# A mixture-of-experts kernel on one core: 64 token tiles in place of 68, the last four with two experts each

## The chip, the cores and the metric

One NeuronCore of one Trainium2 chip. The metric is the device time of one execution in microseconds (us), median of three runs; lower is better.

## The reference

128 samples of 64 tokens and 256 features pass two conditional layers. Each sample names one of 8 experts for the first layer and one of 16 domains for the second. Cut to what matters:

```python
# layer 0: expert of the sample, D=256, I=1024
h = gelu(x[b] @ Wi[e[b]] + bi[e[b]])
r = h @ Wo[e[b]] + bo[e[b]] + x[b]
x = layernorm(r, 1e-12) * gamma[e[b]] + beta[e[b]]
# layer 1: adapter of width 64, domain of the sample
a = gelu(x @ down_W.T + down_b)
a = a @ expert_W[d[b]].T + expert_b[d[b]] + domain_emb[d[b]]
x = layernorm(a @ up_W.T + up_b + x, 1e-5) * ln_gamma + ln_beta
```

## The kernel before

The kernel first sorts the 128 samples on the chip. `count_i`, `two_pairs`, `key`, `place`, `first`, `where` and `slot` (L682 to L698) give every sample a slot so that the samples of one expert are neighbours, the expert with most samples first. A tile is two slots: 128 tokens on the partitions. **Both halves of a tile always have the same expert**, so an expert with an odd count leaves half a tile empty, and the program has a fixed `TILES = B // 2 + E0 // 2` = 68 tiles.

The weights of an expert come from HBM in 8 chunks of 128x512 float32. Each is split into two float16 parts, a high part by ACT (`high`, L518) and a low part by DVE (`low`, L737), and stays in the tiles `W`, at `place` of its expert. Expert 0's chunks are made before the first tile; one more chunk is made per step of the loop after that. A matmul uses high times high, high times low and low times high.

All engines run the same loop of `STEPS = TILES + 5` steps (`run`), each its own part, and wait for each other with semaphores. In step i, PE makes:

- the first product of tile i: 8 blocks `c` of 128 columns of I, 2 halves `k` of D, 3 matmuls each (48 matmuls of 128 moving columns, L929 to L931),
- with it the up product of tile i-4 (L958, L962) and the down product of tile i-3 (L948),
- the second product of tile i-1: L1028 for the bias and 8 blocks `j` times 3 matmuls (24 of 256 moving columns, L937 to L939), and in the middle the transpose of tile i-2 (L970).

ACT makes the Gelu of tile i in 8 blocks (L589), two high parts of it (L597), the turned and scaled `yT` (L629) and the adapter's Gelu (L613, L616). DVE makes the low parts (L775), residual, statistics and normalisation (L785 to L825). POOL makes the inverse roots (L488, L492), the multiplication by gamma (L483), the last scale and shift (L475, L477), and copies the small tables of the tile's expert (`gb_tile` L496, `bi_tile` L461, `sel_tile` L502). SP loads and stores.

Which expert a tile has is known on the chip only. So `W` is read at an address that PE's sequencer works out from registers: at the start of a step it loads four numbers of the tile (`indices`, L262), and `first_addresses` (L918) and `second_addresses` (L923) work out all weight addresses of a few blocks at once, ahead of the matmuls that use them (`pe.lower_ap`):

```python
if c in (1, 3, 5):
    first_addresses(here, range(c + 1, c + 3))
ins = first_product(parity, here, c)
...
    if c in (2, 4):
        second_addresses(there, range(2 * c - 4, 2 * c))
```

In `run`, 8 first steps are written out, 48 steps run in a loop with weights and 8 in a loop without (four steps a turn on PE), and the rest is written out.

Of the kernel before, what the change touches and what calls it, by code (L numbers as in the profile page):

```python
# [9 lines left out]
TILES = B // 2 + E0 // 2  # L10
SLOTS = 2 * TILES
ENTRIES = E1 + 2
# [8 lines left out]
LEAD = NCH  # L21
STEPS = TILES + 5

# [12 lines left out]
IDX_LEN = IDX_CHUNK + E0  # L36


def build(nc, t):
# [4 lines left out]
    with ctx:  # L44
# [36 lines left out]
        bi_tile = sb("bi_tile", [P, 2, KI])  # L81
# [7 lines left out]
        gb_tile = sb("gb_tile", [P, 2 * KD])  # L89
# [38 lines left out]
        before = early(6, SLOTS)  # L128
# [10 lines left out]
        row, empty = early(6, SLOTS)[0:1], early(7, SLOTS)[0:1]  # L139
# [12 lines left out]
        where = early(7, E0)  # L152
        placed = early(7, E0)
# [38 lines left out]
        dst_rows = sem("dst_rows")  # L192
# [39 lines left out]
        yT_done = sem("yT_done")  # L232
        yg_done = sem("yg_done")
# [42 lines left out]
        def run(eng, step, unroll=4, ahead=0):  # L276

            lead, mid = LEAD - ahead, CHUNKS - FIRST_CHUNKS - ahead
# [3 lines left out]
            tail = mid + (TILES - 2 - mid) // 4 * 4  # L282
            for begin, end, weights, times in ((lead, mid, True, unroll), (mid, tail, False, 4)):
                with eng.Fori(0, (end - begin) // times) as n:
                    i = eng.snap(n * times + begin)
                    for q in range(times):
                        step(i + q, q % 2, (begin + q) % 4,
                             (q, n + (FIRST_CHUNKS + LEAD) // NCH, (LEAD + q) % SLOTS_W) if weights else False)
            for i in range(tail, STEPS):
                step(i, i % 2, i % 4, False)  # L290

# [15 lines left out]
        def _(sp):  # L307
            AHEAD = 2
# [12 lines left out]

            def inside(b):
                return [nc.s_assert_within(r, 0, B - 1, skip_runtime_bounds_check_because="the sorting clips every index")
                        for r in b]
# [42 lines left out]
            def step(i, parity, four, weights):  # L367
# [4 lines left out]
                if exists(i + 2) or exists(i - 5):  # L372
                    b = indices(sp, 6 * i + IDX_SP, 6, SLOTS - 1)
                if exists(i + 2):
                    load_turned(inside(b[2:4]), i + 2, parity)
# [5 lines left out]
                if exists(i):  # L381
                    load_natural(inside(b[0:2]), i, parity)

            run(sp, step, NCH, AHEAD)

# [4 lines left out]
        def _(pool):  # L390
# [66 lines left out]

            def gather_bi(e, i, parity):

                need(pool, gelu_half, 2 * i - 2)  # L460
                pool.tensor_copy(bi_tile[:, parity, :], bi_c[:, bass.ds(e * KI, KI)]).then_inc(bi_done, 1)  # L461
# [3 lines left out]
            def step(i, parity, four, weights):  # L465
# [12 lines left out]
                if exists(i - 3):  # L478

                    if isinstance(i, int) and i == 3:  # L480
                        pool.wait_ge(g_in, 16)
                    pool.wait_ge(z1_done, i - 2)
                    pool.tensor_tensor(yg[:, 1 - parity, :], z1[:, :], g_t[:, bass.ds(e_third * D, D)], ALU.mult)\  # L483
                        .then_inc(yg_done, 1)
# [8 lines left out]
                if exists(i - 2):  # L493

                    need(pool, yT_done, i - 2)
                    pool.tensor_copy(gb_tile[:, :], gb_c[:, bass.ds(e_before * 2 * KD, 2 * KD)]).then_inc(gb_done, 1)  # L496
# [19 lines left out]
        def _(act):  # L516
# [64 lines left out]
            def gelu(i, parity, half):  # L581
# [6 lines left out]
                for c in range(half * KI // 2, (half + 1) * KI // 2):  # L588
                    ins = nc.scalar.activation(h[:, c, :], p_h[parity][:, c, :], ACT.Gelu,  # L589
                                               bias=bi_tile[:, parity, c:c + 1], scale=1.0 / (XS * WS))  # L590
                ins.then_inc(gelu_half, 1)

            def high_h(i, parity, half):
# [3 lines left out]
                nc.scalar.activation(h_hi[:, parity, cols_h, :], h[:, cols_h, :], ACT.Copy, scale=HS)\  # L597
                    .then_inc(hhi_half, 1)

            def step(i, parity, four, weights):  # L600
                if exists(i + 1):
                    high_x(i + 1, 1 - parity)
                if weights:

                    act.wait_ge(w_in[weights[2]], w_loads(i, weights[2]))
                    high(weights[0], weights[1], stage[:, weights[2], :]).then_inc(w_hi, 1)
# [11 lines left out]
                if exists(i):  # L618
                    gelu(i, parity, 0)
                    high_h(i, parity, 0)  # L620
# [3 lines left out]
                if exists(i - 2):  # L624
# [3 lines left out]
                    for k in range(KD):  # L628
                        ins = nc.scalar.activation(yT[:, k, :], p_t[:, k * P:k * P + P], ACT.Identity,  # L629
                                                   bias=gb_tile[:, KD + k:KD + k + 1], scale=gb_tile[:, k:k + 1])  # L630
# [7 lines left out]
        def _(dve):  # L638
# [43 lines left out]
            link(v.tensor_scalar(count_i[:, :], p_u[:, 0:E0], 1.0, None, ALU.add))  # L682
# [8 lines left out]
            v.tensor_scalar(idx[:, IDX_CHUNK:IDX_LEN], ord_f[:, :], float(NCH), None, ALU.mult).then_inc(idx_ready, 1)  # L691
# [9 lines left out]
            v.tensor_scalar(before[:, :], iota_r[:, :], slot[:, :], None, ALU.is_gt).then_inc(cols_ready, 1)  # L701
# [23 lines left out]
            n_sort[0] += 4  # L725
# [3 lines left out]
            v.tensor_copy(sel[:, :], p_o[:, 0:SLOTS]).then_inc(sel_ready, 1)  # L729

# [19 lines left out]
            for n, m in enumerate(FIRST_ORDER):  # L750
# [4 lines left out]
                if n == 3:  # L755
# [7 lines left out]
            dve.wait_ge(dst_rows, 1)  # L763
            link(v.tensor_tensor(row, iota_r[0:1, :], p_u[0:1, SLOTS:2 * SLOTS], ALU.subtract))
            link(v.tensor_scalar(empty, p_u[0:1, 0:SLOTS], -1.0, 1.0, ALU.mult, ALU.add))
            link(v.scalar_tensor_tensor(row, row, float(B), empty, ALU.add, ALU.mult))
            v.tensor_tensor(sp_idx[:, 5:TILES + 5, 4:6], row.rearrange("a (t n) -> a t n", n=2),
                            p_u[0:1, 2 * SLOTS:3 * SLOTS].rearrange("a (t n) -> a t n", n=2), ALU.add)\
                .then_inc(idx_ready, 1)

            def split_h(i, parity, half):
# [3 lines left out]
                v.scalar_tensor_tensor(h_lo[:, parity, cols_h, :], h[:, cols_h, :], HS, h_hi[:, parity, cols_h, :],  # L775
                                       ALU.mult, ALU.subtract).then_inc(hlo_half, 1)

            def step(i, parity, four, weights):
# [48 lines left out]
                if weights:  # L827

                    dve.wait_ge(w_hi, i + 1)
                    low(weights[0], weights[1], stage[:, weights[2], :]).then_inc(w_lo, 1)  # L830
# [8 lines left out]
        def _(pe):  # L839
# [36 lines left out]
            pe.wait_ge(cols_ready, 4)  # L876
# [36 lines left out]
            def first_addresses(place_reg, cs):  # L913

                for k in range(KD):
                    for c in cs:
# [171 lines left out]
```

## Time and profile before

| | |
|---|---|
| time, median of 3 runs (lowest to highest) | 499.21 us (498.99 to 499.26) |
| the profiled execution, its own time | 498.85 us |
| its span in the profile | 497.1 us |
| busy: PE, PE weight load, DVE, ACT, POOL | 95%, 88%, 72%, 75%, 72% |
| mean granted TensorE clock | 0.983 of full speed |

Times in rows are microseconds from the start of the span. PEld is the weight load of PE; PEldq, POOLq, ACTq, DVEq and SPq are the sequencers, which do register work and hand instructions to their engines. FUSED_REGOPS and ALU_OP are register instructions, TENSOR_LOAD fetches numbers from memory into registers. "issue" is idle time that no event of another engine explains.

### The profile page before, as it was taken

The numbers are of one execution on the slowest core, as the hardware profiler recorded it, in microseconds if no ns is written. First come the engines' busy times: TensorE is split into PE (matmuls) and PEld (weight loads), VectorE is DVE, ScalarE is ACT, GpSimd is POOL, SyncE is SP. The second block draws the span as 40 slices with busy tenths as digits, with TensorE's granted clock in tenths as the row PEclk, the third lists the DMA queues.
The fourth block names the chain that finished last, engine by engine and source line by source line (L and its number), as shares of the span: only waits on it lengthen the run. The fifth ranks groups of instructions, "written<-read, shape, count | busy, mean of one in ns | idle before, by whom it ended". The sixth has DMA issues, their size and how long they took to land.

```text
span 497.1 us, 19258 instructions
## 1 busy us (share of the span) xinstructions
PE 473.9 (95%) x5778; PEld 438.7 (88%) x5779; DVE 355.6 (72%) x936; ACT 373.8 (75%) x1099; POOL 358.6 (72%) x587
## 2 busy tenths in 40 slices
PE   4699999999999999999999999999999999999972
PEld 2399999999999999999999999999999999999961
DVE  6678777777777777777777777777777767666662
ACT  2588887777787778788777778877878877677651
POOL 6044787788778877788778877887778876667765
PEclk9799999999999999999999999999999999999996
DMA  4734343333343333333333333333343222222111
GB/s 117 269 83 117 93 91 105 100 95 99 102 106 105 86 99 100 98 96 103 103 88 95 99 100 99 102 86 102 97 100 79 63 55 66 64 58 55 39 44 32
DMA packets 70257, 45.84 MB, mean 92 GB/s; under 512 B 43969, under 2 KB 61778, under 8 KB 70098
## 3 DMA queue, kind: packets, MB, share of 16 engines
q1 hardware_dynamic: 69200, 45.25, 34.6%
q8 instruction: 15, 0.25, 0.2%
q10 hardware_dynamic: 1026, 0.21, 0.2%
q14 instruction: 16, 0.13, 0.1%
HBM read 36.51 MB, written 8.91 MB: 91 GB/s over the span
## 4 chain that ended last, share of the span: by engine, by line
PE 93%; DVE 3%; POOL 1%; issue 1%; DMA 0%; ACT 0%; POOLq 0%; DVEq 0%
PE p_h L929 13%; PE p_h L931 12%; PE p_h L930 12%; PE p_o L939 12%; PE p_o L938 12%; PE p_o L937 12%; PE p_d L948 7%; PE p_u L962 6%; PE p_t L970 3%; PE p_u L958 2%; PE p_o L1028 1%; PE p_h L872 1%; DVE W L737 1%; POOL y L475 0%; PE p_t L872 0%
## 5 line engine op out<-in xcount | busy, mean ns | idle before, releaser
L929 PE MATMUL p_h<-x_hi,W 128*128 128x128 f16 x1088 | 193.8, 220 | 0.0
L930 PE MATMUL p_h<-x_lo,W 128*128 128x128 f16 x1088 | 193.6, 220 | 0.0
L931 PE MATMUL p_h<-x_hi,W 128*128 128x128 f16 x1088 | 193.6, 220 | 0.0
L589 ACT ACTIVATE h<-p_h,bi_tile 128x128 f32<-128x128 f32 x544 | 152.6, 362 | 0.6 <-PE p_h L931 0.6
L938 PE MATMUL p_o<-W,h_hi 128*128 x544 | 148.3, 273 | 0.0
L939 PE MATMUL p_o<-W,h_lo 128*128 x544 | 148.3, 273 | 0.0
L937 PE MATMUL p_o<-W,h_hi 128*128 x544 | 148.3, 273 | 0.0
L492 POOL TENSOR_TENSOR rs<-mv,neg_half 128x1 f32<-128x1 f32 x68 | 59.7, 878 | 74.2 <-DVE mv L808 74.2
L929 PEld LDWEIGHTS p_h<-x_hi,W 128*128 x1088 | 107.0, 98 | 5.2 <-issue 3.8
L930 PEld LDWEIGHTS p_h<-x_lo,W 128*128 x1088 | 106.9, 98 | 2.1
L931 PEld LDWEIGHTS p_h<-x_hi,W 128*128 x1088 | 106.9, 98 | 0.0
L613 ACT ACTIVATE a<-p_d,downb 128x128 f32<-128x128 f32 x68 | 25.0, 367 | 90.0 <-PE p_d L948 90.0
L775 DVE SCALAR_TENSOR_TENSOR h_lo<-h,h_hi 128x512 f16<-128x512 f32 x136 | 91.1, 670 | 1.4 <-ACT h_hi L597 1.4
L597 ACT ACTIVATE h_hi<-h 128x512 f16<-128x512 f32 x136 | 86.1, 633 | 2.2
L502 POOL COPY sel_tile<-sel 128x128 f16 (+1 forms) x68 | 81.0, 1191 | 2.0 <-issue 2.0
L805 DVE SCALAR_TENSOR_TENSOR a1s<-a,a1s 64x128 f16<-64x128 f32 x68 | 19.7, 289 | 66.5 <-ACT a1s L616 66.4
L475 POOL TENSOR_TENSOR y<-y,lng 128x256 f32<-128x256 f32 x68 | 49.3, 726 | 20.5 <-DVE h_lo L775 18.7
L785 DVE SCALAR_TENSOR_TENSOR r<-p_o,x_nat 128x256 f32<-128x256 f32 x68 | 28.8, 424 | 44.2 <-PE p_o L939 44.1
L939 PEld LDWEIGHTS p_o<-W,h_lo 128*128 128x128 f16 x544 | 53.2, 98 | 6.2
L938 PEld LDWEIGHTS p_o<-W,h_hi 128*128 128x128 f16 x544 | 53.2, 98 | 6.2
L629 ACT ACTIVATE yT<-p_t,gb_tile 128x128 f32<-128x128 f32 x136 | 55.3, 461 | 3.7 <-PE p_t L970 2.1
L937 PEld LDWEIGHTS p_o<-W,h_hi 128*128 128x128 f16 x544 | 53.2, 98 | 4.7
(155 smaller groups left out, 814.3 us busy)
## 6 DMA issues: line engine op xcount, KB each, us to landing
stage<-in_w SPq DMA_DIRECT2D x56, 256.0 KB, 2.7
x_nat<-in_x SPq DMA_DIRECT2D x136, 64.0 KB, 2.1
out<-y SPq DMA_DIRECT2D x136, 64.0 KB, 2.0
x_T<-in_xT SPq DMA_DIRECT2D x134, 64.0 KB, 2.2
W<-in_w SPq DMA_DIRECT2D x8, 256.0 KB, 4.6
g_t<-in_gamma SPq DMA_DIRECT2D x1, 1024.0 KB, 7.8
W<-in_expert_W SPq DMA_DIRECT2D x2, 128.0 KB, 3.0
upT<-in_up_W SPq DMA_DIRECT2D x2, 64.0 KB, 2.7
```

What stands on the lines that cost most here:

```text
L492: pool.tensor_tensor(rs[:, 1:2], mv[:, 1, 1:2], neg_half[:, 0:1], ALU.pow).then_inc(rs2_done, 1)
L502: pool.tensor_copy(sel_tile[:, four, :].rearrange("p (n s) -> p n s", n=2), sel[:, bass.ds(2 * i, 2)].unsqueeze(2).to_broadcast([P, 2, S]))\
L589: ins = nc.scalar.activation(h[:, c, :], p_h[parity][:, c, :], ACT.Gelu, bias=bi_tile[:, parity, c:c + 1], scale=1.0 / (XS * WS))
L597: nc.scalar.activation(h_hi[:, parity, cols_h, :], h[:, cols_h, :], ACT.Copy, scale=HS)\
L629: ins = nc.scalar.activation(yT[:, k, :], p_t[:, k * P:k * P + P], ACT.Identity, bias=gb_tile[:, KD + k:KD + k + 1], scale=gb_tile[:, k:k ...
L775: v.scalar_tensor_tensor(h_lo[:, parity, cols_h, :], h[:, cols_h, :], HS, h_hi[:, parity, cols_h, :], ALU.mult, ALU.subtract).then_inc(hlo ...
L929: mm(p_h[parity][:, c, :], hi, x_hi[:, parity, k, :], start=(k == 0), stop=False)
L930: mm(p_h[parity][:, c, :], hi, x_lo[:, parity, k, :], start=False, stop=False)
L931: ins = mm(p_h[parity][:, c, :], lo, x_hi[:, parity, k, :], start=False, stop=(k == KD - 1))
L937: mm(p_o[:, 0:D], h_hi[:, parity, j, :], hi, start=False, stop=False)
L938: mm(p_o[:, 0:D], h_hi[:, parity, j, :], lo, start=False, stop=False)
L939: return mm(p_o[:, 0:D], h_lo[:, parity, j, :], hi, start=False, stop=(j == KI - 1))
```

## The change

The tiles become 64. Only whole pairs of one expert are put in the first 60 tiles (`PURE`); the samples that are left over when a count is odd (8 at most) fill the last four tiles (`MIXED`), two samples with an expert each. In those four tiles every operation that depends on the expert is done by halves of 64 tokens. Since fewer tiles come before an expert is needed, each weight chunk is made two steps earlier (`EARLY`), two chunks in each of the first two steps. The output row of a slot is now the row that its input came from, which takes three matmuls and four DVE operations out of the sort.

```diff
-TILES = B // 2 + E0 // 2
+TILES = B // 2
+MIXED = E0 // 2
+PURE = TILES - MIXED
+EARLY = 2
...
-        def run(eng, step, unroll=4, ahead=0):
+        def run(eng, step, unroll=4, ahead=EARLY, first_looped=LEAD):
+            lead, mid = first_looped - ahead, CHUNKS - FIRST_CHUNKS - ahead
...
+            with eng.Fori(0, (mid - lead) // unroll) as n:
...
+            for i in range(mid, STEPS):
                 step(i, i % 2, i % 4, False)
+        def chunks(i, weights):
+            if isinstance(i, int) and i < EARLY:
+                return [(2 * i + q, (2 * i + q, 1, 2 * i + q)) for q in range(2)]
+            return [(i + EARLY, weights)] if weights else []
+        def mixed(i):
+            return isinstance(i, int) and PURE <= i < TILES
+        def tokens(i):
+            return [(n, HALF[n]) for n in range(2)] if mixed(i) else [(0, slice(0, P))]
+        def h_parts(i, parity):
+            if not mixed(i):
+                return h_hi[:, parity, :, :], h_lo[:, parity, :, :]
...  (mixed: two zero-padded copies, in h_hi/h_lo and in the free stage)
         # sort, DVE
+            link(v.scalar_tensor_tensor(excess[:, :], two_pairs[:, :], -2.0, p_u[:, 0:E0], ALU.mult, ALU.add))
+            link(v.tensor_tensor(cube[:, :, :], ahead[:, :, :], rows(excess[:, :], E0), ALU.mult))
+            link(v.tensor_reduce(behind[:, :], cube[:, :, :], AX.X, ALU.add))
+            link(v.tensor_reduce(all_pairs[:, :], two_pairs[:, :], AX.X, ALU.add))
+            link(v.scalar_tensor_tensor(behind[:, :], behind[:, :], all_pairs[:, 0:1], two_pairs[:, :], ALU.add,
+                                        ALU.subtract))
+            link(v.tensor_tensor(left_over[:, :], p_o[:, 0:E0], two_pairs[:, :], ALU.is_ge))
+            link(v.tensor_tensor(left_over[:, :], left_over[:, :], behind[:, :], ALU.mult))
+            link(v.tensor_tensor(where[:, :], where[:, :], left_over[:, :], ALU.add))
-            v.tensor_scalar(before[:, :], iota_r[:, :], slot[:, :], None, ALU.is_gt).then_inc(cols_ready, 1)
         # sort, PE
-            mm(p_u[0:1, 0:SLOTS], cols[:, 1:2], at_slot[:, :], start=True, stop=True)
-            mm(p_u[0:1, SLOTS:2 * SLOTS], cols[:, 1:2], before[:, :], start=True, stop=True)
-            mm(p_u[0:1, 2 * SLOTS:3 * SLOTS], cols[:, 0:1], at_slot[:, :], start=True, stop=True).then_inc(dst_rows, 1)
         # PE
+            def first_addresses(places, cs):
+                if len(places) == 1:
...
+            def second_addresses(places, js):
+                if len(places) == 1:
...
+            def first_product(i, parity, places, c):
+                for n, mine in tokens(i):
+                    for k in range(KD):
+                        hi, lo = first_weights(places[n], c, k)
+                        out = p_h[parity][:, c, mine]
+                        mm(out, hi, x_hi[:, parity, k, mine], start=(k == 0), stop=False)
+                        mm(out, hi, x_lo[:, parity, k, mine], start=False, stop=False)
+                        ins = mm(out, lo, x_hi[:, parity, k, mine], start=False, stop=(k == KD - 1))
+            def second_product(i, parity, places, j):
+                h_high, h_low = h_parts(i, parity)
+                for n, place_n in enumerate(places):
...
+                    mm(p_o[:, 0:D], h_high[at], hi, start=False, stop=False)
+                    mm(p_o[:, 0:D], h_high[at], lo, start=False, stop=False)
+                    ins = mm(p_o[:, 0:D], h_low[at], hi, start=False, stop=(j == KI - 1 and n == len(places) - 1))
+                def places(tile, place_reg):
+                    return indices(pe, IDX_MIX + 2 * (tile - PURE), 2, PLACE_TOP) if mixed(tile) else [place_reg]
+                here, there = places(i, here), places(i - 1, there)
-                        pe.wait_ge(w_lo, i - 1)
+                        pe.wait_ge(w_lo, i + EARLY)
         # POOL
+            def experts(i, e):
+                return indices(pool, IDX_MIX_EXP + 2 * (i - PURE), 2, E0 - 1) if mixed(i) else [e]
...  (used for gamma, bi_tile and gb_tile; gamma in two halves of 64 partitions that wait for each other)
         # ACT, DVE: Gelu, yT, high and low parts in halves for a mixed tile
+                    for n, mine in tokens(i):
+                        ins = nc.scalar.activation(h[:, c, mine], p_h[parity][:, c, mine], ACT.Gelu,
+                                                   bias=bi_tile[:, parity, n, c:c + 1], scale=1.0 / (XS * WS))
+                if isinstance(i, int) and PURE <= i < PURE + 2:
+                    clear_others(i, parity)      # 4 memsets of the zero padding
```

## Rows read from the trace of the kernel before

**Rows 1.** The page: busy us, share of the span, instructions; then its chain.

```profile
PE 473.9 (95%) x5778; PEld 438.7 (88%) x5779; DVE 355.6 (72%) x936; ACT 373.8 (75%) x1099; POOL 358.6 (72%) x587
...
PE 93%; DVE 3%; POOL 1%; issue 1%; DMA 0%; ACT 0%; POOLq 0%; DVEq 0%
```

**Rows 2.** Windows of two steps: length, PE, PEld, DVE, ACT, POOL busy; clock; DMA.

```profile
242.02:248.70 6.68, 6.68 (x87) 6.33 (x85) 4.97 (x13) 5.49 (x17) 5.61 (x9) 1.00 0.36 98
416.40:423.27 6.87, 6.87 (x87) 6.31 (x84) 4.37 (x12) 5.08 (x16) 5.04 (x9) 1.00 0.27 67
```

**Rows 3.** Timeline of PE: start, duration, instruction.

```profile
24.30 0.31 PE L930 MATMUL p_h<-x_lo,W 128*128 128x128 f16 x1
24.41 0.31 PE L931 MATMUL p_h<-x_hi,W 128*128 128x128 f16 x1
...
241.91 0.27 PE L939 MATMUL p_o<-W,h_lo 128*128 x1
242.02 0.22 PE L929 MATMUL p_h<-x_hi,W 128*128 128x128 f16 x1
242.08 0.22 PE L930 MATMUL p_h<-x_lo,W 128*128 128x128 f16 x1
...
416.39 0.10 PEld L929 LDWEIGHTS p_h<-x_hi,W 128*128 x1
...
481.69 0.27 PE L939 MATMUL p_o<-W,h_lo 128*128 x1
```

**Rows 4.** By source line, 413 to 424 us: duration min/median/max ns, first and last start.

```profile
L262 PEldq TENSOR_LOAD <-idx x1: 1003/1003/1003, 414.7 to 414.7; - x1
...
L262 PEldq ALU_OP  x1: 36/36/36, 421.7 to 421.7; - x1
L262 PEldq TENSOR_LOAD <-idx x1: 1000/1000/1000, 421.8 to 421.8; - x1
L918 PEldq FUSED_REGOPS  x3: 60/74/74, 422.9 to 423.2; - x3
L1001 PEldq FUSED_REGOPS  x1: 74/74/74, 423.3 to 423.3; - x1
L929 PEld LDWEIGHTS p_h<-x_hi,W x1: 95/95/95, 423.3 to 423.3; 128*128 x1
```

**Rows 5.** Waits of PE's weight load: us in total, times, longest.

```profile
PEld p_h L929 <- issue: 3.8, 15, 0.7
```

**Rows 6.** By source line, whole run: counts, ns min/median/max.

```profile
L918 PEldq FUSED_REGOPS  x611: 42/74/79, 23.2 to 471.8; - x153
...
L518 ACT ACTIVATE W<-stage x56: 612/628/659, 25.5 to 390.1; 128x512 f32 x48, 128x512 f16<-128x512 f32 x8
L518 ACTq ALU_OP  x42: 35/35/35, 80.2 to 389.0; - x42
...
L518 ACTq FUSED_REGOPS  x6: 60/60/65, 73.6 to 342.3; - x6
...
L262 POOLq TENSOR_LOAD <-idx x71: 562/1174/1281, 13.5 to 484.5; - x71
```

**Rows 7.** Timeline of the sort's end, DVE and PE.

```profile
7.99 0.17 DVE L697 TENSOR_TENSOR W<-W 128x8 f32<-128x8 f32 x1
8.19 0.16 DVE L698 TENSOR_REDUCE slot<-W 128x1 f32<-128x8 f32 x1
...
10.42 1.52 PE L878 MATMUL p_d<-W,cols 128*1 128x136 f32 x6 [1.07 <-DVE W L713]
...
12.62 0.61 PE L882 MATMUL p_u<-W,cols 128*1 128x136 f32 x2
...
14.07 0.80 PE L872 MATMUL p_h<-upT,W 64*128 64x256 f32 x2
```

**Rows 8.** The chain that ended last, around 487 us: start, us, what.

```profile
487.11 0.68 POOL yg L483
487.79 0.89 issue
```

More of the change, by code:

```diff
@@ L152, in build @@
         where = early(7, E0)
+        excess = early(7, E0)
+        behind = early(7, E0)
+        left_over = early(7, E0)
+        all_pairs = early(7, 1)
         placed = early(7, E0)
@@ L281, in run @@
                 step(i, i % 2, i % 4, (j % NCH, (j + FIRST_CHUNKS) // NCH, j % SLOTS_W))
[L282 to L289, printed above, removed]
-                step(i, i % 2, i % 4, False)
+            with eng.Fori(0, (mid - lead) // unroll) as n:
+                i = eng.snap(n * unroll + lead)
+                for q in range(unroll):
+                    step(i + q, q % 2, (lead + q) % 4,
+                         (q, n + (FIRST_CHUNKS + first_looped) // NCH, (first_looped + q) % SLOTS_W))
+            for i in range(mid, STEPS):
+                step(i, i % 2, i % 4, False)
+        def chunks(i, weights):
[9 more added lines that the diff above has]
+                return h_hi[:, parity, :, :], h_lo[:, parity, :, :]
+            if parity:
+                return h_hi, h_lo
+            flat = stage[:, :, :].rearrange("p a b -> p (a b)").bitcast(f16)
+            return [flat[:, u * 2 * KI * P:(u + 1) * 2 * KI * P].rearrange("p (n c q) -> p n c q", n=2, c=KI)
+                    for u in range(2)]
         def loads(i, parity, each):
@@ L495, in step @@
                     need(pool, yT_done, i - 2)
-                    pool.tensor_copy(gb_tile[:, :], gb_c[:, bass.ds(e_before * 2 * KD, 2 * KD)]).then_inc(gb_done, 1)
+                    for n, e_n in enumerate(experts(i - 2, e_before)):
+                        ins = pool.tensor_copy(gb_tile[:, n, :], gb_c[:, bass.ds(e_n * 2 * KD, 2 * KD)])
+                    ins.then_inc(gb_done, 1)
                 if exists(i):
@@ L602, in step @@
                     high_x(i + 1, 1 - parity)
-                if weights:
-                    act.wait_ge(w_in[weights[2]], w_loads(i, weights[2]))
-                    high(weights[0], weights[1], stage[:, weights[2], :]).then_inc(w_hi, 1)
+                for j, (m, place_n, slot_n) in chunks(i, weights):
+                    act.wait_ge(w_in[slot_n], w_loads(j, slot_n))
+                    high(m, place_n, stage[:, slot_n, :]).then_inc(w_hi, 1)
                 if exists(i - 3):
@@ L619, in step @@
                     gelu(i, parity, 0)
+                    if isinstance(i, int) and i == PURE:
+                        act.wait_ge(w_lo, CHUNKS - FIRST_CHUNKS)
                     high_h(i, parity, 0)
@@ L826, in step @@
                                     ALU.subtract, ALU.mult).then_inc(z2_done, 1)
-                if weights:
-                    dve.wait_ge(w_hi, i + 1)
-                    low(weights[0], weights[1], stage[:, weights[2], :]).then_inc(w_lo, 1)
+                for j, (m, place_n, slot_n) in chunks(i, weights):
+                    dve.wait_ge(w_hi, j + 1)
+                    low(m, place_n, stage[:, slot_n, :]).then_inc(w_lo, 1)
+                if isinstance(i, int) and PURE <= i < PURE + 2:
+                    clear_others(i, parity)
                 if exists(i):
@@ L911, in second_weights @@
                 return chunk[:, bass.ds(place_reg + at, D)], chunk[:, bass.ds(place_reg + (at + D), D)]
-            def first_addresses(place_reg, cs):
-                for k in range(KD):
-                    for c in cs:
-                        for part in first_weights(place_reg, c, k):
-                            pe.lower_ap(part, for_matmul_weights=True)
-            def second_addresses(place_reg, js):
-                for j in js:
-                    for part in second_weights(place_reg, j):
-                        pe.lower_ap(part)
@@ new lines, in second_addresses @@
+            def second_addresses(places, js):
+                if len(places) == 1:
+                    for j in js:
+                        for part in second_weights(places[0], j):
+                            pe.lower_ap(part)
+            def first_product(i, parity, places, c):
+                for n, mine in tokens(i):
+                    for k in range(KD):
+                        hi, lo = first_weights(places[n], c, k)
[3 more added lines that the diff above has]
+                        ins = mm(out, lo, x_hi[:, parity, k, mine], start=False, stop=(k == KD - 1))
+                return ins
```

110 lines of the change are left out of this document (60 added, 50 removed).

## The prediction

> **What bounds the kernel now.** I read the page first, then windows of single steps, then PE's instructions one by one, and last the sequencers' own instructions by source line. The page says that PE is busy 95% of the span and carries 93% of the chain that ended last [rows 1]. The windows show how full a step is: 6.68 us, all of it PE, at granted clock 1.00, with DVE, ACT and POOL at 5.0, 5.5 and 5.6 us [rows 2]. In PE's timeline a matmul of 256 moving columns starts 0.109 us after the last one, one of 128 columns 0.055 us after it [rows 3]: columns at full clock and nothing between. So a tile less is 6.68 us less, and four are 26.7 us. What the change is worth hangs on what the four mixed tiles cost.
>
> The instructions by source line show a second stream that is nearly as full, PE's sequencer. At the turn of a loop it does a register instruction at 421.7 us, at 421.8 a load of the tile's numbers, and is not back before 422.9: 1.06 us per load. Three instructions of `first_addresses` follow from 422.9 to 423.2, 0.13 us each, and only at 423.3 comes the first weight load [rows 4]. PE's array hides all of this in a plain step because the sequencer is ahead: the load of a step starts at 414.7 us, and the array gets to that step at 416.39 [rows 3, 4], 1.7 us later. At a loop's turn even that is not enough: that step takes 6.87 us [rows 2], and PE's weight load waits 3.8 us in 15 pieces for "issue" [rows 5]. The trace so shows PE starved by its own sequencer already, by 0.2 us a turn.
>
> **The change, part by part. The plain tiles.** Tiles 0 to 59 stay as they are. `run` has 12 turns on PE where it had 14: -0.4 us at 0.2 a turn. PE's new wait for `w_lo` (i + EARLY) asks for a chunk that DVE makes in step i-1 ahead of the low part of h that PE waits for next, so it never ends last. The second chunk in steps 0 and 1 is 0.63 us more of ACT [rows 6] and about as much of DVE, in steps from which four linked DVE operations go (0.2 us each or more): 0, and 0.6 at most if they were late. SP's transfers stay two steps ahead of their use: 0.
>
> **The start.** DVE gets eight linked operations before `slot`, at the 0.2 us from L697 to L698 [rows 7], and loses one (L701), so L878 on PE starts 1.5 us later than 10.42. Behind it L882 to L884 go, 12.62 to 14.07, 1.45 us [rows 7]. The next link, L872, so starts at about 14.1 as before. +0.1; +1.5 if a late tile of x, which is loaded after the sort, becomes the last to come.
>
> **A mixed tile on PE's array.** Its first product has 96 matmuls of 64 columns where there were 48 of 128. No row shows 64 columns with float16 weights. Below stands half the price of 128, 0.028 us, above the full 0.055. I take 0.028: nothing in the spacing shows a price beside the columns. The second product has 48 matmuls of 256 columns, 5.2 us, where there were 24. With 1.4 us for the rest, the array needs 9.3 us a step (12.0 by the upper bound) where both its tiles are mixed.
>
> **A mixed tile on PE's sequencer.** `first_addresses` and `second_addresses` do nothing for two places. Each weight address is so worked out in front of the matmul that uses it: high and low for 8 blocks, 2 halves of D and 2 experts are 64 in the first product, and 32 in the second. Before, they came in bundles: 611 instructions for 68 x 32 addresses, 3.6 in one [rows 6]. Alone, each takes an instruction. The nearest row of that is ACT's weight conversion, which is not lowered ahead: 42 ALU_OP and 6 FUSED_REGOPS for 48 chunks [rows 6]. The price of one lies between its own duration, 0.036 us, and the 0.133 from one bundle to the next [rows 4]. I take 0.10 us (the light instruction at 421.7 is followed at 421.8; the first block of each expert needs three operations, 0.12): 6.6 us for 64. `places` adds two loads to a step with two mixed tiles, 1.06 us each. Handing over a matmul costs next to nothing, since six pairs pass between the bundle at 423.2 and that of L1001, with which the two are no farther apart than the others [rows 4].
>
> The Trainium skill has two rules here. TensorE: Matmul & The Clock Gate, in its section on the back-to-back issue gap, gives matmuls of 1 to 64 columns some 60 cycles, about 25 ns. The first product of a mixed tile would be 2.4 us by it, if nothing but the array counted; no row here shows such a matmul. Its table also gives TensorE's queue 64 entries, 32 pairs, an estimate of 3.5 us of lead at 0.109; the trace has 1.7 us, and by 3.5 the sum below would come out some 3.5 us lower.
>
> **The sum.** Time 0 is where the array begins step 60 (423.3 us in the trace of before). The sequencer is at -1.7. Step 60: two loads 2.1, 64 addresses 6.6, the addresses of the plain second product 0.6, up product, waits and pairs 0.9: the first product is handed over at 8.5, and the array ends it with it. Its plain second product takes 2.9, so the step ends at 11.4 with the sequencer again 1.7 ahead. Steps 61 to 63: three loads 3.2, 64 addresses 6.6, rest 0.8, together 10.6, then 5.5 for the array's second product; less the lead of 1.7 that is 14.4 a step, 43.3 in all: 54.7. In the second product 32 addresses (3.3) lie under 5.5 of the array. Step 64: two loads and the rest, 2.9 less 1.7, then 5.5: 61.4. In the trace of before the same stretch, to the last second product of tile 67, is 423.3 to 482.0 [rows 3, 4] (the last L939 starts at 481.69 and ends at 482.0): 58.7. So +2.7.
>
> **The end.** After that, the chain runs through POOL [rows 8]. For mixed tiles POOL loads two more numbers for `gb_tile` in the one step and for gamma in the next, 1.17 us each [rows 6], and gamma is two operations of 0.7 in place of one, linked by a semaphore. The load of `gb_tile` puts y L475 off by 1.4, gamma's load shows by some 0.5 behind y L477, the second half by 0.8: +2.7; 0.8 if the loads hid, 4.0 if nothing did.
>
> Total: -0.4 + 0.1 + 2.7 + 2.7 = +5.1 us. The profiled execution took 498.85 us, 1.75 more than its span and 0.36 less than the median; I add to the median: 504.3 us.
>
> **The rivals.** (a) *The addresses are cheap or are hidden*, and the mixed steps go at the pace of another resource. For it speaks that register instructions last 36 to 79 ns and that the whole program shows just 3.8 us of starving [rows 4, 5]; against it, that three bundles and a load starve the array already. POOL would bind: four loads of 1.17, its 5.0 us of a step [rows 2], 0.7 for gamma and an estimated 0.5 for the small copies make 11 us in place of 14.4 in three steps, and step 60 gives 2.5: 12.6 less, 491.7 us. If POOL's loads hid too, the array's 9.3 a step would give 486; its upper bound, 12.0, gives 495. This is the side where the skill's 25 ns would put it. It decides where an address costs less than 0.08 us: 256 addresses in first products, 5.1 us between them and no change.
>
> (b) *The clock falls.* The array works 2.7 of some 10 us while it is fed by addresses. At half clock (0.11 us for 128 columns [rows 3]) the second product takes 10.6, the lead is worth 3.4, a step 17.8: 16 more if it stays so throughout, 520; 512 if it returns half the time. For it speaks that PE's gaps are new, against it that the gaps are short, 0.1 us between one matmul group and the next.
>
> (c) *The forecast's mechanism with another price*: 0.133 an address gives 513, 0.09 gives 502.
>
> **How the numbers follow.** Forecast (sequencer binds at 0.09 to 0.13 us): 0.58, range of its own 499 to 512. Rival (a): 0.29. Rival (b): 0.11, rest 0.02. A change below 0.2% (1 us) is what a measurement of this kernel can't tell. Slower: nearly all of the forecast (0.51) and (b), together 0.62; within 0.2%: 0.05 from the forecast's edge; faster: (a) and the low edge, 0.33. The range 488 to 513 leaves out (a) with all hidden (0.08), the clock down throughout (0.05) and the dearest address (0.04).
>
> **What would show it.** In the profile after: steps 60 to 63 of about 11, 14, 14 and 14 us where plain steps are 6.68; PE and PEld idle for "issue" in groups at L929 to L931's successors, 20 us or more in all; some 64 register instructions per mixed tile at the line of the first weights, 0.1 us apart; PE's share of busy time below 93%; POOL no longer than 11 us in such a step; the chain after the last second product some 3 us longer. Wrong it would be if the mixed steps were 9 to 11 us with POOL or the array without a gap, if the address instructions came bundled, or if the granted clock fell to half in 430 to 485 us.

## The result and the profile after

The changed kernel takes 507.0 us, the median of 4 runs (506.4 to 509.0), against 499.2 us (499.0 to 499.6) of the kernel before on the same chip: a ratio of 1.016 (95% interval 1.014 to 1.017). It is slower, by 7.8 us where 5.1 were forecast. Its profiled execution took 508.95 us with a span of 506.6.

The page of the changed kernel, busy time by engine, the granted clock in 40 slices, and the chain that ended last:

```profile
PE 479.4 (95%) x5724; PEld 437.3 (86%) x5725; DVE 341.7 (67%) x910; ACT 362.5 (72%) x1087; POOL 343.9 (68%) x567
...
PEclk9999999999999999999999999999999999889896
...
PE 90%; DVE 3%; issue 2%; POOL 2%; ACT 2%; DMA 0%; POOLq 0%; DVEq 0%; ACTq 0%
```

PE still looks 95% busy, as before [rows 1], and it has 5.5 us more busy time with 54 matmuls fewer. The slices show what is new: from the 35th on, the clock is no longer whole (the last slice was below whole in the kernel before too).

Windows of the changed kernel tell where the time is (columns as in [rows 2]). The first row is a plain step. The next five run from one step's bias matmul (L1113, between first and second product) to the next, from step 59 to 64; the last row is all that follows the last second product.

```profile
417.54:424.21 6.67, 6.67 (x87) 6.26 (x84) 4.36 (x12) 4.88 (x16) 5.00 (x10) 1.00 0.27 67
...
421.26:433.13 11.87, 11.25 (x135) 9.68 (x133) 7.37 (x22) 6.48 (x23) 6.92 (x14) 0.96 0.21 51
433.13:445.96 12.83, 12.36 (x132) 10.19 (x133) 5.36 (x19) 6.50 (x26) 4.39 (x9) 0.90 0.11 28
445.96:462.08 16.12, 15.38 (x157) 12.76 (x157) 4.96 (x15) 6.50 (x26) 4.83 (x11) 0.90 0.07 18
462.08:476.78 14.70, 13.94 (x156) 12.02 (x157) 4.26 (x13) 6.70 (x26) 4.72 (x10) 0.99 0.08 21
476.78:485.02 8.24, 8.23 (x60) 6.62 (x61) 0.86 (x3) 3.64 (x14) 2.46 (x4) 0.81 0.07 18
...
490.80:506.60 15.80, 4.42 (x25) 2.62 (x25) 6.04 (x18) 2.64 (x8) 8.64 (x15) 0.70 0.14 33
```

Plain steps are what they were. From mark to mark, a step with a mixed first product takes 11.9 to 16.1 us, about twice a plain one. In the one of 16.12 us POOL works 4.83 and ACT 6.50: neither binds. From the start of step 60 (424.21) to the end of the last second product (490.80) it is 66.6 us, against 58.7 before. These 7.9 us are most of the 9.5 by which the two profiled spans differ.

What PE's sequencer did in the mixed tiles, by source line, from 424 us to the end (duration min/median/max ns, first and last start). First the lines of two of the three matmuls, then, for 451 to 453 us, the loads at the start of step 62, one of four numbers and two of two numbers each:

```profile
L1006 PEldq ALU_OP  x95: 32/32/36, 424.3 to 476.3; - x95
L1006 PEldq FUSED_REGOPS  x32: 42/46/51, 424.1 to 472.2; - x32
...
L1008 PEldq ALU_OP  x96: 32/32/32, 424.4 to 476.5; - x96
L1008 PEldq FUSED_REGOPS  x32: 46/46/51, 424.2 to 472.4; - x32
```

```profile
L274 PEldq TENSOR_LOAD <-idx x3: 532/533/1002, 451.2 to 452.8; - x3
```

That is 255 instructions, each in front of one matmul (256 by count, 64 for each mixed tile). What they do to the array is seen in the timeline of PE's weight load in step 62 (start, duration), the first instructions after the three loads:

```profile
453.53 0.10 PEld L1006 LDWEIGHTS p_h<-x_hi,W 128*128 x1 [0.54 <-issue]
453.54 0.10 PEld L1007 LDWEIGHTS p_h<-x_lo,W 128*128 x1
453.65 0.10 PEld L1008 LDWEIGHTS p_h<-x_hi,W 128*128 x1
453.74 0.10 PEld L1006 LDWEIGHTS p_h<-x_hi,W 128*128 x1
453.77 0.10 PEld L1007 LDWEIGHTS p_h<-x_lo,W 128*128 x1
453.86 0.10 PEld L1008 LDWEIGHTS p_h<-x_hi,W 128*128 x1
454.00 0.10 PEld L1006 LDWEIGHTS p_h<-x_hi,W 128*128 x1
```

Three matmuls need two addresses (L1007 uses the weights of L1006). The six from 453.53 to 454.00 take 0.47 us, so an address costs 0.117 us; later in the product it is 0.11. Against that, the first mixed matmuls of step 60, in PE's timeline:

```profile
424.21 0.19 PE L1006 MATMUL p_h<-x_hi,W 128*128 128x64 f16 x1
424.24 0.19 PE L1007 MATMUL p_h<-x_lo,W 128*128 128x64 f16 x1
424.31 0.20 PE L1008 MATMUL p_h<-x_hi,W 128*128 128x64 f16 x1
```

Two matmuls of 64 columns start 0.03 us apart where no address lies between them, half of the 0.055 for 128 [rows 3]; the third waits for its address. At that spacing the array could do a group of three in 0.085 us (an estimate); it gets one every 0.22 to 0.23. Note that each still shows a duration of 0.19 us: durations overlap and fill the gaps, which is why the busy share hides the starving. Starts tell it, durations don't. The list of PE's waits has the same blind spot; of idle time for "issue" it names little more than these:

```profile
PEld p_h L1006 <- issue: 6.0, 20, 0.8
...
PEld p_u L1039 <- issue: 4.0, 8, 1.2
```

And the clock, in the timeline of a second product of 256 columns, where [rows 3] has 0.11 us from one start to the next:

```profile
434.36 0.42 PE L1019 MATMUL p_o<-W,h_lo 128*128 x1
434.57 0.42 PE L1017 MATMUL p_o<-W,h_hi 128*128 x1
```

0.21 us: half clock. In this execution it is so in three stretches of 3.4 us, from 432.2, 445.8 and 476.5 us. Windows of the first one and of the mixed first product ahead of it:

```profile
424.21:432.20 7.99, 7.45 (x99) 6.44 (x98) 4.44 (x14) 3.56 (x14) 3.97 (x9) 1.00 0.18 45
432.20:435.60 3.40, 3.32 (x22) 2.40 (x22) 1.03 (x4) 1.74 (x8) 2.13 (x3) 0.50 0.20 43
```

Each stretch begins 0.2 to 0.9 us ahead of the bias matmul of its step (60, 61 and 63), so near the end of a mixed first product.

The start and the end. In the sort, PE's timeline has

```profile
11.08 0.59 PE L940 MATMUL p_t<-W,cols 128*1 128x128 f32 x2 [3.32 <-DVE W L767]
...
14.73 2.08 PE L947 MATMUL p_h<-upT,W 64*128 64x256 f32 x8
```

where L947 is the L872 of before at 14.07 [rows 7]: +0.7. After the last second product the chain has on POOL (start, duration), and POOL's own timeline beside it:

```profile
492.38 0.55 POOL rs L535
492.93 0.48 issue
493.42 0.51 POOLq L274
```

```profile
493.45 0.61 POOL L539 TENSOR_TENSOR rs<-mv,neg_half 128x1 f32<-128x1 f32 x1 [0.52 <-DVE mv L882]
494.09 0.47 POOL L544 COPY gb_tile<-gb_c 128x4 f32 x2
```

The load of the two experts' numbers for `gb_tile` takes 0.51 us, not 1.17. The chain is led through it, but it ends at 493.93, and POOL is busy with L539 until 494.06, so it delays `gb_tile` by nothing. Gamma's two halves are not in the chain at all. The end is 15.8 us against 15.1.

### The profile page after: what moved, and what is told of

It is laid out like the page before. It is cut to its first block, busy times and chain, and to the rows that moved or that the text cites. A ratio compares the mean times of both kernels' runs of the same rounds, so it can differ in the third digit from the quotient of the medians.

```text
span 506.6 us, 19097 instructions
## 1 busy us (share of the span) xinstructions
PE 479.4 (95%) x5724; PEld 437.3 (86%) x5725; DVE 341.7 (67%) x910; ACT 362.5 (72%) x1087; POOL 343.9 (68%) x567
## 4 chain that ended last, share of the span: by engine, by line
PE 90%; DVE 3%; issue 2%; POOL 2%; ACT 2%; DMA 0%; POOLq 0%; DVEq 0%; ACTq 0%
PE p_h L1006 13%; PE p_h L1008 12%; PE p_o L1017 12%; PE p_o L1018 12%; PE p_o L1019 12%; PE p_h L1007 11%; PE p_d L1029 6%; PE p_u L1043 5%; PE p_t L1051 3%; PE p_u L1039 2%; PE p_o L1113 2%; PE p_h L947 1%; DVE W L810 0%; ACT h L639 0%; ACT ctab L591 0%
## 5 line engine op out<-in xcount | busy, mean ns | idle before, releaser
L1006 PE MATMUL p_h<-x_hi,W 128*128 128x128 f16 (+1 forms) x1088 | 193.3, 216 | 1.3 <-issue 0.8
L1008 PE MATMUL p_h<-x_hi,W 128*128 128x128 f16 (+1 forms) x1088 | 193.3, 216 | 0.0
L1007 PE MATMUL p_h<-x_lo,W 128*128 128x128 f16 (+1 forms) x1088 | 193.1, 216 | 0.0
L639 ACT ACTIVATE h<-p_h,bi_tile 128x128 f32<-128x128 f32 (+1 forms) x544 | 148.7, 359 | 5.3 <-PE p_h L1008 5.3
L1017 PE MATMUL p_o<-W,h_hi 128*128 x512 | 140.2, 274 | 0.0
L1018 PE MATMUL p_o<-W,h_hi 128*128 x512 | 140.1, 274 | 0.0
L1019 PE MATMUL p_o<-W,h_lo 128*128 x512 | 140.0, 273 | 0.0
L1006 PEld LDWEIGHTS p_h<-x_hi,W 128*128 x1088 | 106.4, 98 | 10.0 <-issue 6.0
L1007 PEld LDWEIGHTS p_h<-x_lo,W 128*128 x1088 | 106.3, 98 | 1.9
L539 POOL TENSOR_TENSOR rs<-mv,neg_half 128x1 f32<-128x1 f32 x64 | 55.1, 861 | 73.5 <-DVE mv L882 73.5
L843 DVE SCALAR_TENSOR_TENSOR h_lo<-h,h_hi 128x512 f16<-128x512 f32 (+1 forms) x128 | 83.4, 654 | 1.9 <-ACT h_hi L650 1.8
L650 ACT ACTIVATE h_hi<-h 128x512 f16<-128x512 f32 (+1 forms) x128 | 78.9, 619 | 2.0
L686 ACT ACTIVATE yT<-p_t,gb_tile 128x128 f32<-128x128 f32 (+1 forms) x136 | 54.0, 455 | 12.8 <-PE p_t L1051 10.9
L535 POOL TENSOR_TENSOR rs<-mv,neg_half 128x1 f32<-128x1 f32 x64 | 35.5, 554 | 36.8 <-DVE mv L871 36.8
L1018 PEld LDWEIGHTS p_o<-W,h_hi 128*128 128x128 f16 x512 | 50.3, 98 | 6.1
```

Source lines behind the costliest of these rows:

```text
L539: pool.tensor_tensor(rs[:, 1:2], mv[:, 1, 1:2], neg_half[:, 0:1], ALU.pow).then_inc(rs2_done, 1)
L639: ins = nc.scalar.activation(h[:, c, mine], p_h[parity][:, c, mine], ACT.Gelu, bias=bi_tile[:, parity, n, c:c + 1], scale=1.0 / (XS * WS))
L650: ins = nc.scalar.activation(out, h[:, cols_h, mine], ACT.Copy, scale=HS)
L686: ins = nc.scalar.activation(yT[:, k, mine], turned_z[:, mine], ACT.Identity, bias=gb_tile[:, n, KD + k:KD + k + 1], scale=gb_tile[:, n, k ...
L843: ins = v.scalar_tensor_tensor(lo[at], h[:, cols_h, mine], HS, hi[at], ALU.mult, ALU.subtract)
L1006: mm(out, hi, x_hi[:, parity, k, mine], start=(k == 0), stop=False)
```

## The experiments

Ratios are to the kernel before, with 95% intervals. The marks that bound the windows of steps are always the starts of bias matmuls, as above (steps 59 to 64 in kernels with mixed tiles).

**The addresses in bundles (e1_block).** The changed kernel, but each of 8 blocks of a mixed tile works out its 8 (first product) or 4 (second) addresses together, right ahead of its first matmul.

```diff
             def first_product(i, parity, places, c):
+                if mixed(i):
+                    for n in range(2):
+                        for k in range(KD):
+                            for part in first_weights(places[n], c, k):
+                                pe.lower_ap(part, for_matmul_weights=True)
...
                 h_high, h_low = h_parts(i, parity)
+                if mixed(i):
+                    for place_n in places:
+                        for part in second_weights(place_n, j):
+                            pe.lower_ap(part)
```

> The changed kernel, with the eight weight addresses of a block of a mixed tile worked out together right ahead of the block, so that the register instructions of a mixed step fall from about 100 to 32. Sequencer theory: the first product of a mixed step is handed over some 3.5 us sooner, the three doubly mixed steps take 10 to 11 us in place of 13 to 16, and the kernel takes 493 to 497 us. Theory of the array or of POOL (the addresses are hidden, another resource binds): 507 us as the changed kernel, within 1 us.

Measured: 486.7 us (486.6 to 487.1), ratio 0.975 (0.974 to 0.977). The matmuls, loads and waits are the same: 20.3 us less than the changed kernel, 12.3 less than the kernel before, and below both ranges of the expectation. Windows from the mark of step 60 to that of step 63 of this kernel, and then the instructions by source line in its step 62:

```profile
428.40:435.98 7.58, 7.09 (x139) 6.46 (x136) 5.47 (x19) 6.30 (x26) 4.58 (x10) 1.00 0.19 47
435.98:446.24 10.26, 9.76 (x163) 8.80 (x160) 5.54 (x20) 6.36 (x26) 4.41 (x10) 1.00 0.15 42
446.24:456.64 10.40, 9.74 (x162) 8.85 (x159) 4.69 (x16) 6.53 (x27) 5.19 (x12) 1.00 0.11 28
```

```profile
L1006 PEldq FUSED_REGOPS  x20: 42/74/79, 441.8 to 445.6; - x20
```

20 instructions for 64 addresses, 3.2 in one, against 3.6 in plain tiles [rows 6]. The step is 10.3 us with 4.4 of POOL in it: POOL doesn't bind at 11 us either, and the clock stays whole; both made the expectation too high. The five windows from step 59 to 64 add up to 42.1 us here, to 63.8 in the changed kernel and to 60.1 in e3_wide below, which has the lone addresses at whole clock. So of the 21.7 us between the first two sums, 18.0 are the lone addresses and 3.6 the clock.

**No addresses at all (e2_static).** The mixed tiles use the weights at two fixed places; addresses and the two extra loads fall away.

```diff
-                    return indices(pe, IDX_MIX + 2 * (tile - PURE), 2, PLACE_TOP) if mixed(tile) else [place_reg]
+                    return [0, PLACE] if mixed(tile) else [place_reg]
```

> The changed kernel, with the mixed tiles reading their weights at two fixed places (0 and 1), so that neither addresses nor the two extra loads of numbers are left on PE's sequencer; the matmuls are the same in number and size. What it leaves out: the choice of the expert in the last four tiles. Sequencer theory: all of the mixed steps' excess over the array goes, what binds next is the array at 9.3 us a step or POOL at some 11, 488 to 493 us. Rival (64-column matmuls cost as much as 128-column ones, 0.055 us): 12 us a step, 496 to 499 us. Rival (the half clock is what made the mixed steps long): the clock falls here too and the time stays above 500 us.

Measured: 484.1 us (483.6 to 484.2), ratio 0.970 (0.968 to 0.971), below the expected 488 to 493. Its windows of the same three steps:

```profile
428.25:435.07 6.82, 6.82 (x139) 6.47 (x135) 5.47 (x19) 6.28 (x26) 4.53 (x10) 1.00 0.20 52
435.07:444.51 9.44, 9.44 (x163) 8.82 (x159) 5.54 (x20) 6.35 (x26) 4.40 (x10) 1.00 0.20 52
444.51:453.95 9.44, 9.44 (x163) 8.81 (x159) 4.69 (x16) 6.54 (x27) 5.18 (x12) 1.00 0.12 31
```

With no address and no extra load left, a step with two mixed tiles takes 9.44 us: that is the array's own time. 9.3 was worked out from 0.028 us for 64 columns and the rows of before. In e1_block's timeline twelve such matmuls start one after another:

```profile
425.31 0.19 PE L1011 MATMUL p_h<-x_hi,W 128*128 128x64 f16 x1
...
425.62 0.19 PE L1013 MATMUL p_h<-x_hi,W 128*128 128x64 f16 x1
```

That is 0.31 us for eleven distances, 0.028 each. With the mixed steps at this floor the kernel is 15 us below the kernel before.

**Twice the columns (e3_wide).** The changed kernel, but the first product of a mixed tile runs all 128 columns for both experts, so the array has twice the columns there and the sequencer the same work. It leaves out the first expert's result in these tiles, which the second's overwrites.

```diff
-                        out = p_h[parity][:, c, mine]
+                        out = p_h[parity][:, c, :]
-                        mm(out, hi, x_hi[:, parity, k, mine], start=(k == 0), stop=False)
+                        mm(out, hi, x_hi[:, parity, k, :], start=(k == 0), stop=False)
...
```

> The changed kernel, with all 128 columns in every matmul of a mixed tile's first product: the array's columns there double, the sequencer's work stays. What it changes: the second expert's result overwrites the first's in the mixed tiles. Sequencer theory: three matmuls of 128 columns take 0.17 us and their two addresses 0.23, so the columns are hidden, and the time stays at 507 us, or is up to 5 us less if the fuller array keeps the clock from falling. Array theory: 96 x 0.027 us x 4 tiles = 10 us more, 517 us.

Measured: 505.3 us (505.1 to 505.5), ratio 1.012 (1.011 to 1.014): 1.7 us less than the changed kernel, for more work. Its windows, mark to mark as above for the changed kernel, the second, third and last of the five:

```profile
433.02:444.76 11.74, 11.27 (x132) 9.71 (x133) 5.35 (x19) 6.61 (x25) 4.40 (x9) 1.00 0.13 31
444.76:459.56 14.80, 13.95 (x156) 12.13 (x157) 4.98 (x15) 6.74 (x26) 4.73 (x11) 1.00 0.08 19
...
474.26:481.26 7.00, 6.75 (x61) 5.82 (x62) 1.04 (x3) 3.64 (x14) 2.56 (x4) 1.00 0.09 21
```

11.74, 14.80 and 7.00 us at clock 1.00 stand against 12.83, 16.12 and 8.24 at 0.90, 0.90 and 0.81; the two steps that had clock 0.96 and 0.99 there are the same in both (11.9 and 14.7 us). So the columns of the first product cost nothing, which rules the array out as the bound, and the clock's price in the changed kernel's profiled execution is the difference of the five, 3.6 us. The medians are only 1.7 us apart.

**POOL relieved (e4_pool).** The changed kernel without POOL's extra loads of expert numbers; both halves of gamma and of the small tiles take the first expert's.

```diff
-                return indices(pool, IDX_MIX_EXP + 2 * (i - PURE), 2, E0 - 1) if mixed(i) else [e]
+                return [e, e] if mixed(i) else [e]
```

> The changed kernel without POOL's extra loads of expert numbers in mixed tiles: it uses the number of the tile's first expert for both halves. What it changes: bias, gamma and beta of the second half of the last four tiles. Sequencer theory: POOL is not what binds the mixed steps, only the loads in the chain of the end show, 1 to 2 us less: 505 to 506 us. POOL theory: some 2 us for each of four steps, and the end: 497 us.

Measured: 508.2 us (506.2 to 509.2), ratio 1.019 (1.017 to 1.020): nothing gained, not even the 1 to 2 us expected at the end. In its profiled execution, one of 506.2 us, the clock is at half in two stretches. Ahead of them a window from the mark of step 60 to that of step 61, behind them all that follows the last second product:

```profile
432.60:444.36 11.76, 11.21 (x132) 9.61 (x133) 5.36 (x19) 6.49 (x25) 4.39 (x9) 0.97 0.13 31
443.60:447.00 3.40, 3.38 (x22) 2.44 (x22) 1.04 (x4) 1.74 (x8) 2.13 (x3) 0.50 0.00 0
474.30:477.70 3.40, 3.37 (x20) 2.48 (x21) 0.00 (x0) 1.74 (x8) 2.85 (x4) 0.50 0.08 19
488.58:504.40 15.82, 4.34 (x25) 2.62 (x25) 6.27 (x18) 2.64 (x8) 8.65 (x15) 0.70 0.14 34
```

The first row is a second measure of the clock's price, now with 64 columns as in the changed kernel: the same step takes 11.76 us at clock 0.97, and 12.83 at 0.90. The last row shows that POOL's extra loads cost nothing at the end: it is 15.8 us without them too.

The changed kernel and e4_pool, with half clock in the mixed steps, spread by 2.5 and 3.0 us from run to run, the three above without it by 0.4 to 0.6. A stretch more or less, at 1.0 to 1.3 us each, would do that, but it isn't shown: one execution of each was profiled, and of the changed kernel's four the slowest has the highest mean clock (0.980, the others 0.976 or 0.977).

**The kernel before with lone addresses (e5_alone).** If the price is that of a lone address, plain tiles must pay it too. Here nothing is worked out ahead; each of a tile's 48 addresses is in front of its matmul.

```diff
             def first_addresses(place_reg, cs):
-                for k in range(KD):
...
+                return
             def second_addresses(place_reg, js):
-                for j in js:
...
+                return
```

> The kernel before, with first_addresses and second_addresses doing nothing: every weight address of every tile is worked out alone, in front of its matmul; the array's work, the tiles and the loads are those of before. Sequencer theory: a step then costs the sequencer a load of 1.06 us, 48 addresses at 0.113 us (the spacing in the changed kernel), some 1 us for the other register work and 0.3 for the matmuls, 7.8 us against the array's 6.68; 68 steps give 565 to 585 us. Theory that addresses are hidden when the array is full: 499 to 503 us.

Measured: 573.6 us (573.0 to 573.7), ratio 1.150 (1.148 to 1.152). A plain step, mark to mark, and, by source line in the same window, the addresses of its second product and its load:

```profile
508.45:516.08 7.63, 7.27 (x85) 6.32 (x85) 4.50 (x13) 5.03 (x16) 4.32 (x9) 1.00 0.21 52
```

```profile
L932 PEldq ALU_OP  x6: 32/32/32, 509.0 to 510.2; - x6
L932 PEldq FUSED_REGOPS  x2: 42/46/51, 508.5 to 508.7; - x2
...
L262 PEldq TENSOR_LOAD <-idx x1: 997/997/997, 510.5 to 510.5; - x1
```

7.63 us where it was 6.67, with the array's work unchanged. The 16 addresses of the second product (L932 and L933, 8 each) take from 508.5 to 510.4, 0.12 each: the price found in mixed tiles. 48 at 0.115 are 5.5, the load is 1.0, together 6.5; the remaining 1.1 are the rest of the step, not measured by themselves. The array's own 6.7 us no longer covers that.

**The start (e6_start), the loads ahead (e7_early_loads), and both (e8_all).** All on top of e1_block. The first converts two chunks a step in steps 2 and 3 in place of 0 and 1; for that, SP also issues the chunk's load behind that of the tokens in steps 0 to 3, so it changes two things at once. The second has PE load the next step's numbers in the middle of the second product, not at the step's start, and keeps the place that it already has, so that its first load is of two numbers and not of four:

```diff
-            if isinstance(i, int) and i < EARLY:
-                return [(2 * i + q, (2 * i + q, 1, 2 * i + q)) for q in range(2)]
+            if isinstance(i, int) and i < 2 * EARLY:
+                return [(j, (j, 1, j % SLOTS_W)) for j in ((0,), (1,), (2, 3), (4, 5))[i]]
...
                         ins = second_product(i - 1, 1 - parity, there, j)
+                        if j == KI // 2 and isinstance(i, int) and PURE - 1 <= i < TILES:
+                            taken_ahead.append(numbers(i + 1, here))
```

> As e1_block, and the two extra weight chunks are made in steps 2 and 3 in place of steps 0 and 1. Theory that the second conversion delays ACT and DVE in the first two steps, which were not full of slack as the prediction had it: 1 us less than e1_block, 485.7 us. Rival (the later start comes from the longer sort): as e1_block, 486.7 us.

> As e1_block, and PE's sequencer loads the numbers of the next step of a mixed tile in the middle of the second product, where the array has 5.5 us of work and the sequencer 1.5, in place of two or three loads at the start of the step. Sequencer theory: the first products no longer wait for loads, 2 to 3 us less than e1_block, 484 us, and steps with two mixed tiles at the array's 9.4 us. Rival (the rest of the excess is the bundles or POOL): 486 to 487 us.

> e6_start and e7_early_loads together. If the two causes are separate their gains add: 483 us, 3.2% faster than the kernel before and 4.8% faster than the changed one.

Measured: 485.9 us (485.3 to 486.6), ratio 0.974 (0.973 to 0.976); 483.5 us (483.4 to 483.7), ratio 0.969 (0.968 to 0.970); 483.1 us (482.6 to 483.5), ratio 0.968 (0.967 to 0.970). The start alone is 0.8 us below e1_block with overlapping intervals: not settled. Nor do the traces settle it: in e6_start the bias matmul of step 3 is at 44.48 us, as in the kernel before (44.52), but in e8_all, with the same start, at 45.73. The loads give 3.2 us; the step of two mixed tiles in e7_early_loads is

```profile
434.99:444.43 9.44, 9.44 (x162) 8.82 (x159) 5.54 (x20) 6.36 (x26) 4.40 (x10) 1.00 0.20 52
```

the same 9.44 as with fixed places, so in such a step addresses and loads are now wholly hidden. The two loads of this step, by source line, are of two numbers each:

```profile
L274 PEldq TENSOR_LOAD <-idx x2: 532/540/549, 436.7 to 437.3; - x2
```

The first of the two, too, takes 0.55 us and not 1.0. So what a load costs on PE went with how many numbers it fetches, not with its place in the row. e8_all is the best version: 16 us (3.2%) below the kernel before, 4.7% below the changed one.

## Why the prediction was right, point by point

The direction and the mechanism were right. That the total came so near is in part luck, as the terms below show. And one of the signs that the prediction itself named as being wrong did appear: the granted clock fell to half between 430 and 485 us.

**What bounds the mixed steps: right.** It is the sequencer, not the array (e3_wide: twice the columns, no dearer) and not POOL (e4_pool). The lone address is the cause: e1_block changes nothing else in the program and takes 20.3 us away, and e5_alone puts the same price on plain tiles.

**The plain tiles: right,** 6.67 us as before. The turns were to give 0.4 back, and gave 0.2 at most: the mark of step 3 is 1.1 us later than before (45.60 against 44.52), the array's entry into step 60 is 0.9 later.

**The start: +0.1 forecast, 1.1 measured by the mark of step 3.** The step that failed is "The next link, L872, so starts at about 14.1 as before". The eight linked DVE operations moved L940 from 8.74 (as L865) to 11.08 us, 2.3 and not the 1.5 that the prediction took, and 0.7 of it reached L947. By the mark of step 1 just 0.2 is left of that (33.03 against 32.84; the clock was at half from 22 to 26 us before, and whole after), and another 0.9 arises from there to the mark of step 3. The second doubled pair of chunks lies in step 1; that it is the cause wasn't shown (e6_start, e8_all).

**The mixed stretch: +2.7 forecast, +7.9 measured.** Four terms differ:
- The price of an address, taken at 0.10, is 0.113 to 0.117: at 0.115, 256 of them are 3.8 us more.
- The loads, 1.06 each in the sum, are so only where four numbers are fetched; the extra ones fetch two, last 0.53 (once 0.72), and the next starts 0.6 after them. A row of three takes 2.1 to 2.4 where 3.2 was forecast, about 3.5 us less over the stretch.
- The clock: 3.6 us, worked out with e3_wide. It was rival (b), given 0.11, and came in beside the forecast's mechanism, not in place of it: three stretches of 3.4 us, where (b) had 13 to 21 us more than no change. The prediction held against it that the gaps are short; they were, and it fell all the same.
- What is left, 7.9 less 2.7, 3.8 and 3.6, plus 3.5, is 1.3 us, 0.3 a step, of changes of block, waits and other products between the addresses; 0.8 a step was allowed for them. That is a remainder, not measured by itself.

The forecast step of 14.4 came out at 14.7 to 14.8 where the clock stayed up, since two of the errors cancel.

**The array's share: right.** 9.3 forecast, 9.44 in e2_static; half of 0.055 for 64 columns. The Trainium skill (TensorE: Matmul & The Clock Gate, on the back-to-back issue gap) gives about 25 ns for 1 to 64 columns. The starts 0.03 us apart agree. The same section of the Trainium skill says that in streams of weight load and matmul the sustained spacing for 128 columns is about 81 ns; here it is 0.055 [rows 3], and the measurement decides.

**The end: +2.7 forecast, +0.7 measured.** The step that failed is that POOL's extra loads and gamma's second half lie in the chain, at 1.17 us a load. The extra load takes 0.51 and hides beside L539, gamma's halves lay beside the chain, and e4_pool ends in the same 15.8 us without the loads. What the 0.7 is made of wasn't separated; `yT` L686 now takes 1.29 us in four pieces where L629 took 0.81 in two.

**Rival (a), POOL at 11 us: fell.** Even where the addresses are bundled, POOL does not bind: such steps take 10.3 us in e1_block. Had the addresses been hidden, the array's 9.44 would have bound, and the result would have been about 484 (e2_static), near the 486 of the rival's second variant.

**The signs named in advance.** Steps of 11, 14, 14, 14 us: 11.9, 12.8, 16.1, 14.7 by marks (12.8 and 16.1 with the fallen clock in them). Addresses 0.1 us apart, 64 a tile: yes. PE and PEld idle for "issue" 20 us or more, PE's share below 93%: no, 10 us and 95%, though the starving was as large as forecast. Those two were the wrong views: matmuls that overlap cover gaps of 0.1 us with their own durations.

**Total.** 0.9 ahead of step 60, 7.9 in the stretch and 0.7 at the end make the 9.5 us between the two spans; the medians are 7.8 apart, since the profiled execution was the slowest of its four. So the forecast of +5.1 missed by 2.7 against the medians and by 4.4 against the profiled executions. In the latter, start, addresses, clock and remainder came out 9.9 us dearer than forecast, loads and end 5.5 cheaper: that these partly cancel was luck. The direction was not: e3_wide, whose clock did not fall, is still slower than the kernel before (1.012).

## What to carry to other kernels

Where an operand's address comes from a register, the sequencer's work is a stream of its own beside the array's: count its instructions for each step and set them against the array's time. An address worked out alone in front of its matmul cost 0.115 us, three in a bundle 0.13 together, so smaller matmuls on dynamic addresses starved the array here until the addresses were bundled and the loads of numbers moved under a long product. And read the spacing of starts, not the busy share: this PE was 95% busy over the run, while in the mixed first products it got little more than a third of the matmuls that it could take.

## What the runs showed of the hardware

- A load on PE's sequencer took 1.0 us where it fetched four numbers and 0.53 to 0.55 where it fetched two, first in its row (e7_early_loads) or behind another (changed kernel). On POOL the extra loads of two numbers took 0.5 to 0.52; the step's own of five numbers took 1.17 in most steps and about 0.6 in some (rows 6 has 0.56 as the least), which wasn't explained.
- The granted clock fell to half although PE was nearly always busy by the records: 7.45 of the 7.99 us ahead of the first fall and 3.32 of the 3.40 in it. Ahead of each fall PE had a mixed first product of some 8 us, a group of three 64-column matmuls every 0.22 to 0.23 us. With 128 columns in place of 64 in the same groups, at the same pace of instructions, it stayed at full (e3_wide, one execution); so it did from step 59 to 64 with the bundled addresses (e1_block). All five falls, three in the changed kernel and two in e4_pool, begin 0.2 to 0.9 us ahead of the bias matmul of their step. Both kernels have one in steps 61 and 63, only the changed kernel in step 60, and neither in step 62, whose first product looks the same. The Trainium skill (TensorE: Matmul & The Clock Gate, "A second HAM failure mode: psum-queue depth-cycling") tells of a kernel with matmuls of 512 columns whose clock oscillates because PE idles very briefly and often between groups of matmuls. This case is alike in that no long idle time is needed; whether the cause is the same, and why the clock fell in one mixed step and not in the next, wasn't settled.
- Doubling the columns of a starved product made the kernel 1.7 us faster by the medians (505.3 against 507.0).
